# Attention outputs turned by DMA copies and normalised once an element, in place of transposes on TensorE; weights loaded after the first stacks

## The chip, the cores and the metric

The kernel runs on one core of one Trainium2 chip. The metric is the time of one execution on the device in microseconds (us). Beside it stand the times of several runs of the kernel before, and one execution that the hardware profiler recorded.

## What is computed

Eight elements (b) each go through a grouped-query cross attention and then through a recurrent block. Cut to what matters here:

```python
# attention: x (8,256,256), ctx (8,1601,256); 32 query heads, 8 key heads, 8 channels a head
q = (x @ Wq + bq).reshape(b, l, 8, 4, 8).transpose(0, 2, 3, 1, 4)
k = (ctx @ Wk + bk).reshape(b, s, 8, 8).transpose(0, 2, 1, 3)      # v in the same way
scores = einsum('bkgld,bksd->bkgls', q, k) / sqrt(8) + mask
attn = softmax(scores, axis=-1)
out = einsum('bkgls,bksd->bkgld', attn, v).transpose(0, 3, 1, 2, 4).reshape(b, l, 256)
x = layernorm(out @ Wo + bo + x) * gamma + beta
# block: layer norm, token shift, five mixes, r k v w g, a scan over 256 tokens
#   s = k v^T + w s   (32 heads of 8x8),  o = r (u k v^T + s),
# group norm, gate, Wo, layer norm, and a gated square-relu feed-forward
```

## The kernel before, in words

**Stages.** Elements are pipelined. `elements(it, lo)` gives for each turn `it` of the outer loop the elements f = it+2 (its context and queries are projected), a = it+1 (its values are turned, its keys and queries are stored to DRAM and loaded back as stacks), b = it (its scores, exponentials and weighings), c = it-1 (output projection and the first part of the recurrent block) and d = it-2 (feed-forward). There are ten turns; the first has no c, in the last two no b. On each engine the order of the work in a turn is written out by hand; a turn has STEPS = 52 steps.

**Scores.** A step is one chunk of 128 keys (13 chunks) of one of four groups of eight heads. Per step TensorE makes two tiles of scores (`score_tile`), ScalarE takes their exponentials (`exp_tile`, 128x1024) and TensorE weighs them (`weigh`) into the one accumulator bank `po`: four products with `v_aug`, which has the 8 value channels and a column of ones for each of four key heads, so that rows 32j to 32j+7 of `po` are the weighed values of head j and row 32j+8 is the sum of the exponentials. In light steps (LIGHT, and all but two where there is no c) a weighing stands between two score tiles; in the others both weighings of the pair of steps stand together. Side work of the other elements is put behind each even step (`side`, `score_rows`).

**The output of a group.** At the end of each group (steps 13, 26, 39 and, for the last, step 0 of the next turn) VectorE copies `po` to `o_raw` (`keep_output`); the first weighing of the next group waits for it (`o_kept`). TensorE turns `o_raw` to rows of tokens with four transposes (`turn_output`, at steps 22, 28 and 42, and at step 0 of the next turn), and VectorE takes the reciprocals of the 16 sums and multiplies (`norm_output`: one reciprocal and four products) into `attn`. At step 2 of the next turn `attn` is turned back to channels by four transposes (`turn_rows`), VectorE copies it to `attn_t`, and at step 4 `product_rows(attn_t, w_o, ...)` is the output projection.

**VectorE's order around step 26.** State passes 0 to 3 of the recurrence (`state_pass`, a product and a scan each), the copy of r, `keep_output(b, 1)`, `rk`, state pass 4, `norm_output(b, 1)`, g, passes 5 and 6, `bias_kv(f, 0)`, pass 7. The key projections of element f are at steps 30, 32, 40 and 40 (`project_kv`); the second waits for `bias_kv(f, 0)`, since both use one bank.

**The SP queue.** SP issues nearly all DMAs, in this order in a turn: step 0 second half of the stacks of b and x_rows of c; step 4 the stores of the queries (12) and keys (6) of a; 12 the output; 14 the shift of b to DRAM and back; 18 `spread_v(c)`, eight transfers of 257 KB that repeat each value channel over a head; 20 `load_ctx(f)` (four) and `load_x_t(f)`; 26 the first stacks of a; 38 the shift of a; 44 the mask of f. Each of these waits for what it needs, and what stands behind it waits too.

**The start.** `project` on ScalarE, with VectorE, splits keys and queries of element 0 in three bf16 parts; SP stores the keys and one half of the queries, ACT's queue the other half (`store_queries`), and both load half of the first stack. Then come a short scoring round, the shift to DRAM and back, and the first scores. SP loads the context and x of element 1 as soon as those of element 0 are projected. GpSimd issues 46 loads of weights (`late`) once the first context has landed; they are first needed in the second turn.

## Time and profile before

| | |
|---|---|
| median of 3 runs | 1179.3 us (1173.62 to 1179.63) |
| profiled execution | 1178.83 us |
| its span, first to last instruction | 1176.9 us |
| TensorE (PE) busy | 1054.9 us, 90% |
| ScalarE (ACT) busy | 860.3 us, 73% |
| VectorE (DVE) busy | 574.8 us, 49% |
| GpSimd (POOL) busy | 309.0 us, 26% |
| mean granted TensorE clock | 0.952 |

The shares are averages over a start of some 56 us without scores, eight turns with scores, and a tail in which the last element goes on alone. An engine's busy time counts compute instructions only. The chain that ended last lies on TensorE for 62% of the span, on ScalarE for 23%, on VectorE for 5% and on DMAs for 3%.

### The profile page before, as it was taken

The numbers are of one execution on the slowest core, as the hardware profiler recorded it, in microseconds if no ns is written. First come the engines' busy times: TensorE is split into PE (matmuls) and PEld (weight loads), VectorE is DVE, ScalarE is ACT, GpSimd is POOL, SyncE is SP. The second block draws the span as 40 slices with busy tenths as digits, with TensorE's granted clock in tenths as the row PEclk, the third lists the DMA queues.
The fourth block names the chain that finished last, engine by engine and source line by source line (L and its number), as shares of the span: only waits on it lengthen the run. The fifth ranks groups of instructions, "written<-read, shape, count | busy, mean of one in ns | idle before, by whom it ended". The sixth has DMA issues, their size and how long they took to land.

```text
span 1176.9 us, 18264 instructions
## 1 busy us (share of the span) xinstructions
PE 1054.9 (90%) x7181; PEld 376.0 (32%) x7181; DVE 574.8 (49%) x1095; ACT 860.3 (73%) x940; POOL 309.0 (26%) x356
## 2 busy tenths in 40 slices
PE   3198999999999999999999999999997999888777
PEld 2031223333333233323333333323331333224413
DVE  5031215464448445555547453844555364635562
ACT  2078988889878887888788988887788888881110
POOL 9221051232314041314123231314132012300330
PEclk8599999999999999999999999999999999998766
DMA  8534133631536140904253143614070225000400
GB/s 258 128 82 134 25 83 86 93 83 57 116 44 136 59 95 30 170 6 94 83 87 88 58 113 44 139 59 93 31 107 3 34 75 82 3 1 9 72 0 13
DMA packets 65374, 87.48 MB, mean 74 GB/s; under 512 B 8208, under 2 KB 48192, under 8 KB 65280
## 3 DMA queue, kind: packets, MB, share of 16 engines
q1 hardware_dynamic: 61728, 81.22, 31.6%
q0 software_dynamic: 2176, 4.11, 1.5%
q8 instruction: 59, 0.97, 0.3%
q10 hardware_dynamic: 1376, 0.90, 0.3%
q14 instruction: 35, 0.29, 0.1%
HBM read 50.74 MB, written 18.62 MB: 59 GB/s over the span
## 4 chain that ended last, share of the span: by engine, by line
PE 62%; ACT 23%; issue 6%; DVE 5%; DMA 3%; SPq 1%; POOL 0%; ACTq 0%; DVEq 0%; POOLq 0%
PE psum L795 61%; ACT probs L738 19%; DMA vs<-v_c 1%; DMA q_stacked<-q_parts 1%; ACT L738 1%; ACT L770 1%; PE psum L885 1%; SPq L291 1%; DVE xa L1336 1%; DMA q_stack<-q_stacked 1%; DVE row_max L1248 1%; DVE sx L1341 0%; ACT xm L767 0%; ACT xm L770 0%; SPq L367 0%
## 5 line engine op out<-in xcount | busy, mean ns | idle before, releaser
L738 ACT ACTIVATE probs<-psum 128x1024 f32<-128x1024 f32 (+1 forms) x832 | 798.9, 1022 | 199.8 <-PE psum L795 197.5
L795 PE MATMUL psum<-probs,v_aug 128*9 128x512 f32 (+1 forms) x3328 | 416.7, 599 | 1.3 <-DVE o_raw L1296 1.2
L795 PE MATMUL psum<-q_stack,k_stack 64*128 64x512 bf16 (+1 forms) x1745 | 320.5, 395 | 50.2 <-ACT probs L738 37.9
L795 PEld LDWEIGHTS psum<-q_stack,k_stack 64*128 64x128 bf16 (+1 forms) x1745 | 81.9, 96 | 440.5 <-ACT probs L738 359.5
L795 PEld LDWEIGHTS psum<-probs,v_aug 128*9 128x9 f32 (+1 forms) x3328 | 61.6, 89 | 161.2 <-issue 151.3
L599 POOL TENSOR_TENSOR vs<-r_c,vs 128x512 f32<-128x512 f32 x64 | 86.5, 1361 | 96.4 <-DVE tmp L1523 53.9
L576 POOL TENSOR_TENSOR xm<-tmp,xa 128x512 f32<-128x512 f32 x40 | 43.5, 1104 | 233.2 <-DVE tmp L1356 233.2
L1369 DVE TENSOR_TENSOR_SCAN vs<-w_c,vs 128x514 f32<-128x514 f32 x64 | 90.1, 1408 | 21.8 <-POOL vs L590 19.9
L563 POOL TENSOR_TENSOR rstd<-moments,eps 128x2 f32<-128x2 f32 x24 | 4.7, 195 | 255.8 <-DVE moments L1322 255.8
L1296 DVE COPY o_raw<-psum 128x512 f32<-128x512 f32 x32 | 21.9, 684 | 89.7 <-PE psum L795 89.7
L1362 DVE TENSOR_TENSOR vs<-k_c,vs 128x512 f32<-128x512 f32 x64 | 61.9, 967 | 0.3
L1356 DVE SCALAR_TENSOR_TENSOR tmp<-psum,chan,sx 128x256 f32<-128x256 f32 x80 | 33.5, 478 | 53.3 <-PE psum L795 53.3
L795 PE MATMUL psum<-ctx_t,w_kv 128*128 128x400 f32 (+1 forms) x128 | 50.1, 529 | 5.4 <-DMA ctx_t<-in_ctx_t 5.4
L535 POOL CAST k_parts<-kv 64x1601 bf16<-64x1601 f32 x7 | 10.6, 1519 | 121.0 <-DVE kv L1225 121.0
L1248 DVE TENSOR_REDUCE row_max<-psum 128x16 f32<-128x512 f32 x32 | 20.6, 684 | 41.8 <-PE psum L795 41.8
L1225 DVE TENSOR_SCALAR kv<-psum,b_kv 128x400 f32<-128x400 f32 (+1 forms) x28 | 17.6, 627 | 42.5 <-PE psum L795 42.5
L795 PE MATMUL psum<-k_stack,q_stack 48*128 48x32 bf16 x512 | 9.0, 174 | 30.9 <-DMA q_stack<-q_stacked 30.9
L795 PEld LDWEIGHTS psum<-ctx_t,w_kv 128*128 128x128 f32 x128 | 23.3, 195 | 25.2 <-issue 11.1
L1566 DVE RECIPROCAL xm<-xm 128x512 f32<-128x512 f32 x8 | 26.8, 3348 | 7.1 <-ACT xm L770 7.1
L1242 DVE TENSOR_REDUCE mask_max<-ctx_t 128x1 f32<-128x1601 f32 x16 | 28.7, 1806 | 0.0
L795 PE MATMUL psum<-mix,w 128*128 128x256 f32 (+1 forms) x64 | 18.0, 415 | 6.2 <-DVE mix L1345 6.2
L1285 DVE CAST shift_parts<-psum 32x128 bf16<-32x128 f32 x16 | 4.5, 279 | 38.8 <-PE psum L795 38.8
(181 smaller groups left out, 1061.8 us busy)
## 6 DMA issues: line engine op xcount, KB each, us to landing
vs<-v_c SPq DMA_DIRECT2D x61, 257.0 KB, 7.6
ctx_t<-in_mask SPq DMA_DIRECT2D x8, 1601.0 KB, 6.7
k_stacked<-k_parts SPq DMA_DIRECT2D x48, 200.1 KB
ctx_t<-in_ctx_t SPq DMA_DIRECT2D x24, 400.0 KB, 6.1
k_stack<-k_stacked SPq DMA_DIRECT2D x31, 300.2 KB, 6.6
q_stack<-q_stacked SPq DMA_DIRECT2D x31, 192.0 KB, 7.1
q_stacked<-q_parts SPq DMA_DIRECT2D x90, 64.0 KB, 3.1
ctx_t<-in_ctx_t SPq DMA_DIRECT2D x8, 401.0 KB, 6.4
```

Of the source, the lines that this page charges most:

```text
L576: nc.gpsimd.tensor_tensor(xm[MIX_ORDER[n]][:, :, :], tmp[n % 2][:, :, :], xa[:, :, 1:L + 1], ALU.add)\
L599: nc.gpsimd.tensor_tensor(vs[:, j, :, 0:L], r_c[:, :, :], vs[:, j, :, 0:L], ALU.mult)\
L738: nc.scalar.activation(probs[turn_step % NP][t][0:w, :, :], ps[t][0:w, :, :], ACT.Exp).then_inc(exped.sem, 1)
L795: return nc.tensor.matmul(dst, lhsT, rhs, start=start, stop=stop)
L1225: nc.vector.tensor_scalar(kv32[:, at:at + w], bank(at_bank)[:, 0:w], b_kv[:, 0:1], None, ALU.add)\
L1242: nc.vector.tensor_reduce(mask_max[:, a, lc:lc + 1], ctx_t[:, lc, :], AX.X, ALU.max, apply_absolute_value=True).then_inc(mask_seen.sem, 1)
L1248: last = nc.vector.tensor_reduce(row_max[:, :].rearrange("p (r a u) -> p r a u", a=2, u=4)[:, :, half, :], bank(6 + half).rearrange("p (r ...
L1296: nc.vector.tensor_copy(o_raw[:, :], po).then_inc(o_kept.sem, 1)
L1356: last = nc.vector.scalar_tensor_tensor(tmp[n % 2][:, e, :], halves(at)[:, e, :], vec(f"s{f}", e), sx[:, e, :], ALU.add, ALU.mult)
L1362: nc.vector.tensor_tensor(vs[:, j, :, 1:L + 1], k_c[:, :, :], vs[:, j, :, 1:L + 1], ALU.mult)\
L1369: nc.vector.tensor_tensor_scan(flat, w_c[:, :, :].rearrange("p e l -> p (e l)"), flat, 0.0, ALU.mult, ALU.add)\
L1566: link(nc.vector.reciprocal(std_o[:, :, :], std_o[:, :, :]))
```

## The change

1. `turn_output`, `norm_output`, the turning of `attn` and the copy to `attn_t` go. After each `keep_output`, SP copies each head's eight rows of `o_raw` to `attn_t`, laid by channels, and its row of sums, repeated eight times, to `den_t` (`turn_attn`: eight DMAs a group, at steps 22, 30 and 42, and the last at step 0 of the next turn, ahead of the stacks).
2. VectorE normalises once an element, at the head of the turn (`norm_attn`: a reciprocal, a minimum for the check of small sums, and a product, all 128x512), and the output projection at step 4 waits for it.
3. `keep_output` of a group waits for the copies of the group before it out of `o_raw`.
4. Waits on TensorE that stood for the removed work are put on what is next in those banks. LIGHT gets steps 22 and 28.
5. x_rows is loaded at step 46 of the turn before. `w_o` is loaded in eight pieces in the new order of channels.
6. At the start, the 53 loads of weights are issued after the first stack has landed, and the context and x of element 1 after SP's half of the first stack. Of the second half of the queries, two of six stores go to ACT's queue.

```diff
-LIGHT = (2, 8, 10, 18, 38, 42, 48)
+LIGHT = (2, 8, 10, 18, 22, 28, 38, 42, 48)
+ATTN_STEP = (22, 30, 42)
+FIRST_STORES = 2
...
+            wo_attn = c["L0_xattn_Wo"].rearrange("(g j u h d) n -> g u h j d n", g=GQ, j=4, u=2, h=GQ)
+            for group in range(GROUPS):
+                for h in range(GQ):
+                    yield w_o[32 * group:32 * group + 32, h, :], wo_attn[group // 2, group % 2, h]
...
+            def turn_attn(b, group):
+
+                if group == 0 and b > 0:
+                    sp.wait_ge(wo_done.sem, wo_done.at(b - 1))
+                sp.wait_ge(o_kept.sem, o_kept.at(b, group + 1))
+                for j in range(4):
+                    p0 = 32 * group + HD * j
+                    for dst, src in ((den_t, o_raw[32 * j + HD:32 * j + HD + 1, :].rearrange("p (a n) -> p a n", a=1)
+                                      .broadcast_to([1, HD, 512])),
+                                     (attn_t, o_raw[32 * j:32 * j + HD, :])):
+                        sp.dma_start(dst[p0:p0 + HD, :, :].rearrange("p h l -> p (h l)"), src).then_inc(attn_in.sem, 16)
...
-                sp.wait_ge(kv_proj.sem, kv_proj.at(lo))
-                load_ctx(lo + 1)
-                sp.wait_ge(q_proj.sem, q_proj.at(lo))
-                load_x_t(lo + 1)
...
                 store_k_parts(lo)
-                store_q_parts(lo, (1,))
+                sp.wait_ge(q_low.sem, q_low.at(lo))
+                store_queries(sp, lo, 1, range(FIRST_STORES, NR))
                 load_stacks(lo, 0, (0,))
+                sp.wait_ge(kv_proj.sem, kv_proj.at(lo))
+                sp.wait_ge(q_proj.sem, q_proj.at(lo))
+                load_ctx(lo + 1)
+                load_x_t(lo + 1)
...
                         if step == 0:
+                            if c is not None:
+                                turn_attn(c, 3)
                             if b is not None:
                                 load_stacks(b, 1)
-                            if c is not None:
-                                load_x_rows(c)
+                        if step in ATTN_STEP and b is not None:
+                            turn_attn(b, ATTN_STEP.index(step))
+                        if step == 46 and b is not None:
+                            load_x_rows(b)
...
+                if lo == 0:
+                    pool.wait_ge(stack_in[0].sem, stack_in[0].at(0))
+                    for dst, src in late:
+                        pool.dma_start(dst, src).then_inc(late_in.sem, 16)
...
-            pool.wait_ge(ctx_in[NK - 1].sem, ctx_in[NK - 1].at(0))
-            for dst, src in late:
-                pool.dma_start(dst, src).then_inc(late_in.sem, 16)
...
                 store_queries(act, a, 0)
+                store_queries(act, a, 1, range(FIRST_STORES))
...
             def keep_output(b, group):
                 dve.wait_ge(weighed.sem, weighed.at(b, NC * (group + 1)))
-                dve.wait_ge(o_turned.sem, o_turned.at(b, group))
+                if group > 0:
+                    dve.wait_ge(attn_in.sem, attn_in.at(b, 16 * HD * group))
+                elif b > 0:
+                    dve.wait_ge(attn_in.sem, attn_in.at(b - 1))
                 nc.vector.tensor_copy(o_raw[:, :], po).then_inc(o_kept.sem, 1)
...
+            def norm_attn(b):
+
+                dve.wait_ge(attn_in.sem, attn_in.at(b))
+                nc.vector.reciprocal(den_t[:, :, :], den_t[:, :, :]).then_inc(den_turned.sem, 1)
+                dve.wait_ge(den_turned.sem, den_turned.at(b))
+                nc.vector.tensor_reduce(den_low[:, b % B:b % B + 1], den_t[:, :, :], AX.XY, ALU.min)
+                nc.vector.tensor_tensor(attn_t[:, :, :], attn_t[:, :, :], den_t[:, :, :], ALU.mult)\
+                  .then_inc(attn_normed.sem, 1)
```

## Rows read from the trace of the kernel before

**Rows 1.** Windows, one element: us, busy (instructions) of each engine, clock, DMA share, GB/s

```profile
371.96:499.62 127.66, 123.59 (x888) 44.77 (x889) 69.94 (x137) 106.64 (x117) 34.85 (x37) 1.00 0.38 83
```

**Rows 2.** Groups of instructions by shape, whole span: busy us, mean ns, idle before

```profile
L885 PE MATMUL psum<-ident,o_raw 128*128 128x128 f32 x128 | 20.6, 283 | 0.4 <-DVE o_raw L1296 0.4
...
L1310 DVE TENSOR_TENSOR attn<-psum,r_den 128x32 f32<-128x32 f32 x128 | 15.5, 184 | 1.1
...
L1303 DVE RECIPROCAL r_den<-psum 128x16 f32<-128x16 f32 x32 | 7.8, 245 | 31.0 <-PE psum L885 31.0
...
L891 PE MATMUL psum<-ident,attn 128*128 128x128 f32 x32 | 5.2, 286 | 1.8 <-DVE attn L1310 1.8
```

**Rows 3.** Timeline of TensorE in one element: start us, us, what

```profile
379.30 1.61 PE L795 MATMUL psum<-ctx_t,w_kv 128*128 128x400 f32 x4
...
406.46 0.39 PE L795 MATMUL psum<-q_stack,k_stack 64*128 64x512 bf16 x2 [0.22 <-ACT probs L738]
...
438.29 1.99 PE L795 MATMUL psum<-w_o,attn_t 128*128 128x256 f32 x8
...
484.40 0.66 PE L885 MATMUL psum<-ident,o_raw 128*128 128x128 f32 x4
484.99 0.70 PE L795 MATMUL psum<-q_stack,k_stack 64*128 64x512 bf16 x4
...
495.30 1.91 PE L795 MATMUL psum<-probs,v_aug 128*9 128x512 f32 x16
```

**Rows 4.** Timeline of VectorE in the same element

```profile
378.57 0.61 DVE L1225 TENSOR_SCALAR kv<-psum,b_kv 128x401 f32<-128x401 f32 x1
...
401.34 3.34 DVE L1566 RECIPROCAL xm<-xm 128x512 f32<-128x512 f32 x1
...
427.70 0.69 DVE L1296 COPY o_raw<-psum 128x512 f32<-128x512 f32 x1 [4.39 <-PE psum L795]
...
440.75 0.69 DVE L1460 TENSOR_TENSOR x<-psum,x_rows 128x512 f32<-128x512 f32 x1 [2.30 <-PE psum L795]
...
492.56 0.68 DVE L1296 COPY o_raw<-psum 128x512 f32<-128x512 f32 x1
```

**Rows 5.** Timeline of the SP queue in the same element

```profile
469.88 14.85 SPq L304 DMA_DIRECT2D vs<-v_c  x8
484.85 4.73 SPq L351 DMA_DIRECT2D ctx_t<-in_ctx_t  x4
489.62 0.58 SPq L354 DMA_DIRECT2D x_t<-in_x_t  x1
```

**Rows 6.** DMA issues from 470 to 498 us: KB each, us to landing

```profile
x_t<-in_x_t SPq DMA_DIRECT2D x1, 256.0 KB, 7.6
```

**Rows 7.** DMA issues of the whole span: count, KB each, median us to landing

```profile
q_stacked<-q_parts SPq DMA_DIRECT2D x90, 64.0 KB, 3.1
...
shift_stacked<-shift_parts SPq DMA_DIRECT2D x16, 24.0 KB, 1.4
```

**Rows 8.** Timeline of all engines at the start, 0 to 62 us

```profile
10.85 0.93 POOL L681 DMA_DIRECT2D w_o<-in_L_xattn_Wo  x1 [0.32 <-POOL q_stack L677]
...
19.76 4.10 ACTq L291 DMA_DIRECT2D q_stacked<-q_parts  x6
...
22.89 8.75 SPq L291 DMA_DIRECT2D q_stacked<-q_parts  x6
...
35.86 0.54 POOL L681 DMA_DIRECT2D s_init<-in_s_init  x1
...
39.85 0.35 SPq L284 DMA_DIRECT2D k_stack<-k_stacked  x1
...
47.02 0.61 PE L795 MATMUL psum<-k_stack,q_stack 48*128 48x32 bf16 x32 [30.92 <-DMA q_stack<-q_stacked]
...
51.28 0.30 SPq L385 DMA_DIRECT2D shift_stacked<-shift_parts  x1
...
56.12 1.04 PE L795 MATMUL psum<-q_stack,k_stack 64*128 64x512 bf16 x4 [6.25 <-issue]
```

**Rows 9.** Timeline of all engines where the last element's scores end

```profile
1065.17 0.69 DVE L1296 COPY o_raw<-psum 128x512 f32<-128x512 f32 x1 [3.60 <-PE psum L795]
...
1070.66 3.78 PE L795 MATMUL psum<-w_o,attn_t 128*128 128x256 f32 x8 [0.78 <-DVE attn_t L1452]
```

More of the change, by code:

```diff
@@ L880, in weigh @@
                 last.then_inc(weighed.sem, 1)
-            def turn_output(b, group, to):
-                pe.wait_ge(o_kept.sem, o_kept.at(b, group + 1))
-                for u in range(4):
-                    last = nc.tensor.transpose(bank(to)[:, P * u:P * u + P], o_raw[:, P * u:P * u + P], ident[:, :])
-                last.then_inc(o_turned.sem, 1)
             def turn_rows(x, to, done):
@@ L1124, in side @@
                         if n == 0:
-                            pe.wait_ge(o_normed.sem, o_normed.at(b, 2))
+                            if c is not None:
+                                pe.wait_ge(k_ready.sem, k_ready.at(c))
+                            else:
+                                pe.wait_ge(v_kept.sem, v_kept.at(a))
                         elif n == 1:
@@ L1508, in all_turns @@
                         mix_of(c, 4)
-                    if b is not None:
-                        norm_output(b, 0, 6)
                     if c is not None:
@@ L1526, in all_turns @@
                         state_pass(c, 4)
-                    if b is not None:
-                        norm_output(b, 1, 5)
                     if c is not None:
@@ L1573, in all_turns @@
                           .then_inc(og_ready.sem, 1)
-                    if b is not None:
-                        norm_output(b, 2, 5)
                     if c is not None:
```

83 lines of the change are left out of this document (17 added, 66 removed).

## Prediction

> **What bounds the kernel now.** I read the busy time by stretch first, one stretch per element, then the waits inside one, then the timelines of TensorE, VectorE, the SP queue, and last the start and the end. One element takes 127.66 us, in which TensorE is busy 123.59 and ScalarE 106.64, at a granted clock of 1.00 [rows 1]. So TensorE sets the pace, with short stretches in which it waits for an exponential instead, as in [rows 3] before 406.46. The reader is to see two kinds of time there: a TensorE instruction taken out of the first kind is worth its length, one out of the second is worth nothing. The program's own time for the profiled execution is 1178.83 us, the span 1176.9; the sum below is made against 1178.83, which lies 0.5 under the median of the runs, 1179.3.
>
> Names: "round 1 to 5" are the turns of the outer loop in which an element's scores, the tail of the one before and the projection of the one two ahead all run; rounds 6 and 7 lack the projection; the first turn is round 0; the tail follows round 7. Steps of one round lie as in [rows 3]: step 0 near 425, step 28 near 495, steps 30 and 32 near 375 and 379 (add 127.66 to set them behind step 28).
>
> **Turning removed from TensorE.** Four blocks of four transposes of o_raw and one block of attn an element: 128 cost 20.6 us and 32 cost 5.2 [rows 2], 0.64 us a block, and the timeline advances by about 0.53 where a block goes. The blocks at steps 0, 22 and 28 stand where TensorE is never idle (the one at 484.40 is followed at once by scores, [rows 3]): 3 x 0.53 = 1.6 us an element. The blocks at steps 2 and 42 are followed by a wait for ScalarE (the one before 406.46), so they give nothing. In round 0, with light steps only, I take nothing. Steps 22 and 28 become light; their side work falls to about 1.1 us, and the finer order only makes sure that the 0.53 is reaped. Bound: 0 to 0.3 more a step. Without any new wait this is 1.6 in each of seven rounds.
>
> **Normalising on VectorE.** Removed: 4 x (0.245 + 4 x 0.121) [rows 2] and one copy of 0.69, together 3.6 us an element. Added, all at once at the head of a round: a reciprocal of 128x512, 3.34 us by the one at 401.34, a minimum and a product of that width, 0.69 each by the 440.75 one [rows 4]: 4.7 us. VectorE has room for it (busy 69.94 of 127.66, [rows 1]); what matters is who waits.
>
> **The head of a round (steps 0 to 4).** o_raw is copied at 427.70 to 428.39 [rows 4]. SP must then issue eight DMAs of 16 KB (8 partitions of 512 f32). No such copy is in the trace; the nearest issue rows are 0.30 us (51.28) and 0.35 us (39.85) and, for sixteen-partition ones, 0.68 (six in 4.10) [rows 8]; I take 0.4, which gives 431.7. Landing: 1.4 us by the shift rows, 3.1 by the query stores [rows 7]; with the queue else empty I take 2 from the start of the last issue, 433.3. Then 4.7 on VectorE: 438.1. TensorE wants attn_t at 438.29 - 0.53 = 437.8 [rows 3], so it waits 0.4 and the step-0 gain shrinks to 0.1. Bounds: issue 0.3 and landing 1.4 leave no wait; 0.68 and 3.1 give 3.7 us of wait each round. Behind the waiting product stands all of TensorE's queue. x0's addition (440.75) and what follows it keep their time, since SP's later items, the loads of the second stacks and eighteen stores, move by some 8 us where they have 10 or more to spare.
>
> **The copies at step 22: the heart of the forecast.** The first group's o_raw is ready early in the round, but SP runs in order, and its copies stand behind the eight spread transfers (469.88, 14.85 us of issuing) and the loads of the next context and x (484.85 and 489.62) [rows 5]. So the first of the eight is issued at 490.2, the last near 493.6. The second group's keep_output is now made to wait for them, and before it ran at 492.56 [rows 4]. The load of x issued at 489.62 took 7.6 us to land, at 497.2 [rows 6]. If the small copies queue behind it they land near 497.6: VectorE is late by 5.0 us. Behind keep_output there stand rk, state passes 4 to 7 and the bias of the next keys; behind rk, GpSimd's products. TensorE wants the freed accumulator for the weighing at 495.30 [rows 3], minus 0.5 to 0.8 by the gains and the lighter step; it stops until 498.3, 3.5 us. The second half of VectorE's lateness shows at step 32: the key projection at 379.30 [rows 3] waits for the bias that ends at 378.57 + 0.61 = 379.18 [rows 4], 0.12 us before it. VectorE has lost 5.0 and saved one norm_output since (0.7), so that bias comes 4.4 later, and TensorE, its gains at 22 and 28 swallowed, is 4.3 later than before. Lower bound: copies that land 2 us after the last issue, 495.5, make VectorE late by 2.9 and the round 2.1 longer. Upper: landing at 499.5 gives 6.2. I take 4.3, as the nearest row is a transfer on the same queue issued 0.6 us earlier. In rounds 6 and 7 no context is loaded: copies are issued from 484.85 and, 7.6 behind the last spread issue near 482.9, land near 490.5, in time, and steps 22 and 28 gain 0.5 each. In round 0 nothing is spread and there is no wait.
>
> By the page "DMA: Bandwidth & Descriptors" of the Trainium skill, section "Queues, rings and completion order", each engine takes the descriptors of a ring in order, yet "completion is not FIFO per issuing engine", and a DMA uses at most sixteen rings. The trace has landings in order of issue, but no copy of eight partitions. Were these small copies to overtake, the rounds would cost the 2.1 of the lower bound and the sum would be that of rival B.
>
> **The other copies.** Groups 1 and 2 are asked for half a round after they are issued, and x_rows moves to step 46, all with over 10 us to spare: nothing.
>
> **The start.** The first scores come at 56.12 [rows 8]. Before that the query stores on SP take 8.75 us for six, where ACT's six took 4.10 (0.68 each), while GpSimd's loads run until 35.86 + 0.54; the stack loads go out at 39.85 and are used at 47.02. After: SP has four stores and ACT eight, so both are issued by 22.9 + 2.7 = 25.6; landing 3.1 [rows 7] gives 28.7, 11.1 us sooner. The stacks then share the engines with the next context, behind SP's half: 1 us lost. The round trip of the shift (51.28 to 56.12, 4.8 us) now meets that context and the late weights: 0.6 us lost. Gain 9.5; bounds 4 and 12. GpSimd's 53 loads (0.55 each, as 46 ran from 10.85 to 36.4 [rows 8]) start near 36.5 and end near 66, before q_scaled lets it go on near 69: hidden; without that cover they cost nothing until the stores of step 8 are late by over 5 us.
>
> **The tail.** No score work covers the last element. o_raw is copied by 1065.86, the product ran at 1070.66 [rows 9]. After: 8 x 0.4 + 1.6 + 4.7 + 0.1 = 9.6 (terms as at the head of a round), so 1075.5: 4.8 lost, bounds 3.5 and 8. The flag check loses two 512-wide instructions, hidden behind the spread.
>
> **Sum.** Start -9.5; round 0, 0; rounds 1 to 5, 5 x (4.3 - 0.1) = +21; rounds 6 and 7, 2 x (-1.0 - 0.1) = -2.2; tail +4.8. Together +14.1: 1178.8 + 14.1 = 1193.
>
> **Rivals.**
> A, faster: no wait at step 22, because the DMAs land before 492.6. It is decided at that point: with SP issuing from 490.2 it needs the spread or the context to be issued 3 us faster than in [rows 5]. -9.5 - 7 x 1.1 + 4.8 = -12.4: 1166.
> B, a short wait: the copies land 2 us after their issue, despite the context. -9.5 + 5 x (2.1 - 0.1) - 2.2 + 4.8 = +3.1: 1182.
> C, the start gives little: late weights delay the shift's two hops and the stacks, gain 4 rather than 9.5: 1198.
> D, the head of the round becomes a wait too: issue at 0.68 and landing 3.1 add 3.3 to each of seven rounds: 1216. The order of SP speaks against: nothing is queued ahead then.
>
> **Chances.** Forecast 0.46, A 0.18, B 0.19, C 0.10, D 0.07. Within 0.5% is about what a measurement of this kernel can tell from no change: 1173.4 to 1185.2. Faster is A with a little of B (0.20); same is most of B and the low edge of the forecast (0.20); slower 0.60. The range 1166 to 1203 takes in B, C, the upper stall of 6.2 (1203) and half of A; the forecast's own is 1185 to 1203.
>
> **What would show it.** o_raw's second copy in a round on VectorE should follow a DMA, 4 to 6 us of idle; TensorE idle before the first weighing of group 2, about 3.5 us, and at the key projection of step 32, under 1; five rounds near 131.9 us, then two near 126.5. The first scores should start near 46.5. The last attn_t product should come some 10 us after o_raw. If the rounds are 126.5 throughout, the queue argument is wrong; if the first scores come after 52, the start is.

## Result and the profile after

The changed kernel takes 1224.05 us (median, 1221.41 to 1225.63), the kernel before, run beside it, 1179.47. The ratio is 1.0383, interval 1.0351 to 1.0415: slower by 3.8%. Forecast was 1193.0 with a range to 1203: the sign was right, the size a third of what came (14.1 us for 42.3 between the two profiled executions, 44.6 between the medians). The profiled execution of after took 1221.41 us with a span of 1219.2, 42.3 more than the span before.

First the windows of one element (round 3), cut at VectorE's four copies into `o_raw`; columns as in [rows 1]:

```profile
440.84:477.04 36.20, 31.54 (x249) 11.93 (x249) 23.17 (x45) 27.93 (x32) 6.03 (x8) 1.00 0.43 96
477.04:512.95 35.91, 32.38 (x214) 12.88 (x214) 14.97 (x24) 27.43 (x31) 7.01 (x7) 0.99 0.64 120
512.95:545.54 32.59, 31.27 (x220) 7.76 (x220) 18.60 (x25) 24.82 (x27) 11.94 (x12) 0.90 0.22 34
545.54:576.15 30.61, 29.05 (x190) 10.18 (x190) 15.31 (x27) 26.56 (x29) 11.23 (x10) 1.00 0.21 67
```

The same four stretches of before, 427.70 to 555.36, are 34.60, 30.26, 32.19 and 30.61 us long. The element has grown from 127.66 to 135.31, and the growth sits in two stretches: the first one, where VectorE normalises, and above all the second, which ends when the second copy into `o_raw` can start.

That second stretch on the SP queue:

```profile
484.61 14.76 SPq L306 DMA_DIRECT2D vs<-v_c  x8
499.49 4.95 SPq L356 DMA_DIRECT2D ctx_t<-in_ctx_t  x4
504.48 0.55 SPq L359 DMA_DIRECT2D x_t<-in_x_t  x1
505.13 0.86 SPq L416 DMA_DIRECT2D den_t<-o_raw  x1
...
510.14 0.63 SPq L416 DMA_DIRECT2D attn_t<-o_raw  x1
```

and who waits for it, on VectorE and then on TensorE:

```profile
506.65 0.67 DVE L1498 COPY r_c<-psum 128x512 f32<-128x512 f32 x1
512.95 0.69 DVE L1291 COPY o_raw<-psum 128x512 f32<-128x512 f32 x1 [5.63 <-DMA attn_t<-o_raw]
```

```profile
509.28 0.39 PE L819 MATMUL psum<-q_stack,k_stack 64*128 64x512 bf16 x2
513.79 1.89 PE L819 MATMUL psum<-probs,v_aug 128*9 128x512 f32 x8 [4.11 <-DVE o_raw L1291]
```

The eight copies of the first group stand behind spread, context and x, as forecast from [rows 5]; each holds SP for 0.63 us and they start 0.67 apart. The x just ahead of them was issued at 504.48 and took 7.6 us to land, so it landed at 512.1 (DMA issues, 495 to 520: KB each, us to landing):

```profile
x_t<-in_x_t SPq DMA_DIRECT2D x1, 256.0 KB, 7.6
```

The copies landed by 512.95, 2.8 us behind the start of the last issue. VectorE's wait is 5.40, 5.85, 5.63, 4.82 and 4.87 us in rounds 1 to 5 (forecast 5.0), and 1.35 and 1.30 in rounds 6 and 7 (forecast none). TensorE's stop is 3.88, 4.33, 4.11, 3.30 and 3.35 us in rounds 1 to 5 (forecast 3.5). In rounds 4 and 5 TensorE waits once more, for the bias of the keys at step 32, as the prediction had it (forecast under 1); here round 4:

```profile
661.52 1.61 PE L819 MATMUL psum<-ctx_t,w_kv 128*128 128x400 f32 x4 [0.22 <-DVE kv L1217]
```

The head of the round, on VectorE:

```profile
440.84 0.69 DVE L1291 COPY o_raw<-psum 128x512 f32<-128x512 f32 x1 [4.39 <-PE psum L819]
...
448.30 3.35 DVE L1296 RECIPROCAL den_t<-den_t 128x512 f32<-128x512 f32 x1 [3.61 <-DMA attn_t<-o_raw]
```

and on TensorE, behind the minimum and the product that follow it:

```profile
453.03 1.99 PE L819 MATMUL psum<-w_o,attn_t 128*128 128x256 f32 x8 [1.96 <-DVE attn_t L1299]
```

SP's issues run from 441.56 to 446.93 and the reciprocal starts at 448.30: 2.0 us behind the start of the last issue, as assumed, but eight issues took 5.4 us and not 3.2. So here too TensorE stops, 1.96 us a round where 0.4 was forecast; 3.02 in round 1 and 2.45 in round 7.

The clock of TensorE in the stop and behind it (windows; columns as in [rows 1]):

```profile
509.00:513.00 4.00, 0.67 (x4) 0.10 (x2) 0.05 (x1) 1.27 (x2) 0.00 (x0) 0.94 0.53 142
513.00:515.00 2.00, 1.21 (x8) 0.16 (x8) 2.00 (x4) 0.00 (x0) 0.49 (x1) 0.50 1.14 191
515.00:517.00 2.00, 2.00 (x12) 0.26 (x12) 0.03 (x1) 0.73 (x1) 2.00 (x2) 0.50 1.13 178
517.00:519.00 2.00, 2.00 (x11) 0.16 (x3) 1.56 (x1) 1.70 (x3) 2.00 (x4) 0.50 0.96 129
```

After the stop of round 3 the granted clock is 0.50 (1.2 of 2.4 GHz) for some seven microseconds, and a block of eight weighings takes 1.89 us instead of 1.05. Behind the stops of rounds 1, 2, 4 and 5 half clock lasts some three and a half microseconds, and so it does behind TensorE's wait at the head of rounds 1, 2 and 7, where it follows waits of 3.02, 1.96 and 2.45 us; behind the waits of 1.95 and 1.96 us at the head of rounds 3 to 6 there is none. Before has no such stretch in its rounds 1 to 5. It looks like a second bill for the same stop, and nothing in the prediction speaks of it. The third experiment is about it.

The start, on TensorE:

```profile
38.67 0.61 PE L819 MATMUL psum<-k_stack,q_stack 48*128 48x32 bf16 x32 [21.45 <-DMA q_stack<-q_stacked]
...
50.92 1.04 PE L819 MATMUL psum<-q_stack,k_stack 64*128 64x512 bf16 x4 [9.41 <-issue]
```

The first stack is used 8.35 us sooner than in [rows 8], but the first scores come only 5.2 us sooner: the round trip of the shift, 4.8 us in [rows 8], now takes 8.0. The tail ends as follows (TensorE, the last element; the answer to [rows 9]); the last copy into `o_raw` began at 1104.02:

```profile
1116.19 3.78 PE L819 MATMUL psum<-w_o,attn_t 128*128 128x256 f32 x8 [10.31 <-DVE attn_t L1299]
```

Where the 42.3 us are, read from the starts of the fourth copy into `o_raw` of each element in the two traces:

```
                                 before            after            change   forecast
start and round 0 (to its copy)  174.60            169.47            -5.1     -9.5
rounds 1 to 5                    810.84 - 174.60   843.37 - 169.47   +37.7    +21
rounds 6 and 7                   1065.17 - 810.84  1104.02 - 843.37   +6.3    -2.2
tail                             1176.9 - 1065.17  1219.2 - 1104.02   +3.5    +4.8
```

Every row but the last missed on the side that makes the time longer.

### The profile page after: what moved, and what is told of

The parts are those of the page before. It is cut to its first block, busy times and chain, and to the rows that moved or that the text cites. A ratio compares the mean times of both kernels' runs of the same rounds, so it can differ in the third digit from the quotient of the medians.

```text
span 1219.2 us, 18031 instructions
## 1 busy us (share of the span) xinstructions
PE 1049.5 (86%) x7021; PEld 358.4 (29%) x7021; DVE 589.9 (48%) x951; ACT 860.3 (71%) x940; POOL 322.2 (26%) x363
## 4 chain that ended last, share of the span: by engine, by line
PE 46%; ACT 18%; issue 11%; SPq 9%; DVE 9%; DMA 4%; POOL 1%; ACTq 1%; POOLq 0%; DVEq 0%
PE psum L819 46%; ACT probs L762 15%; SPq L416 4%; SPq L306 4%; DVE den_t L1296 2%; DMA attn_t<-o_raw 2%; SPq L356 1%; DMA vs<-v_c 1%; ACT L762 1%; ACT L794 1%; DVE o_raw L1291 1%; ACTq L293 1%; DVE xa L1322 1%; DVE vs L1348 1%; DMA q_stack<-q_stacked 1%
## 5 line engine op out<-in xcount | busy, mean ns | idle before, releaser
L819 PE MATMUL psum<-probs,v_aug 128*9 128x512 f32 (+1 forms) x3328 | 427.3, 609 | 20.3 <-DVE o_raw L1291 20.2
L1355 DVE TENSOR_TENSOR_SCAN vs<-w_c,vs 128x514 f32<-128x514 f32 x64 | 102.3, 1598 | 21.9 <-POOL vs L612 20.0
L598 POOL TENSOR_TENSOR xm<-tmp,xa 128x512 f32<-128x512 f32 x40 | 46.0, 1166 | 235.0 <-DVE tmp L1342 235.0
L1348 DVE TENSOR_TENSOR vs<-k_c,vs 128x512 f32<-128x512 f32 x64 | 54.6, 853 | 0.3
L819 PE MATMUL psum<-w_o,attn_t 128*128 128x256 f32 x64 | 20.9, 481 | 25.6 <-DVE attn_t L1299 25.6
L1296 DVE RECIPROCAL den_t<-den_t 128x512 f32<-128x512 f32 x8 | 26.8, 3353 | 32.6 <-DMA attn_t<-o_raw 32.6
L1217 DVE TENSOR_SCALAR kv<-psum,b_kv 128x400 f32<-128x400 f32 (+1 forms) x28 | 17.6, 627 | 50.7 <-PE psum L819 50.7
L1546 DVE RECIPROCAL xm<-xm 128x512 f32<-128x512 f32 x8 | 26.8, 3347 | 7.1 <-ACT xm L794 7.1
L819 PE MATMUL psum<-k_stack,q_stack 48*128 48x32 bf16 x512 | 9.0, 174 | 21.5 <-DMA q_stack<-q_stacked 21.5
```

The source lines that it names most:

```text
L598: nc.gpsimd.tensor_tensor(xm[MIX_ORDER[n]][:, :, :], tmp[n % 2][:, :, :], xa[:, :, 1:L + 1], ALU.add)\
L819: return nc.tensor.matmul(dst, lhsT, rhs, start=start, stop=stop)
L1296: nc.vector.reciprocal(den_t[:, :, :], den_t[:, :, :]).then_inc(den_turned.sem, 1)
L1348: nc.vector.tensor_tensor(vs[:, j, :, 1:L + 1], k_c[:, :, :], vs[:, j, :, 1:L + 1], ALU.mult)\
L1355: nc.vector.tensor_tensor_scan(flat, w_c[:, :, :].rearrange("p e l -> p (e l)"), flat, 0.0, ALU.mult, ALU.add)\
```

## The experiments

The theory after this reading: the order of the SP queue makes the wait behind step 22; copies at 0.63 us each to issue make the wait at the head; the half clock behind the stop costs another 2 us a round; the shift's round trip at the start is slow by what is loaded beside it. Times are medians beside the kernel before on the same chip, whose median in the four series was 1177.97, 1178.45, 1178.93 and 1178.47 us. "First stretch" to "fourth stretch" of a round are those of the windows above. In rounds 1 to 5 of after they last 36.2 us (36.93 in round 1, 37.78 in round 2), 35.1 to 36.1, 31.7 to 31.9 (32.59 in round 3) and 30.60.

**1. The copies of the first group ahead of the spread.**

```
-ATTN_STEP = (22, 30, 42)
+ATTN_STEP = (16, 30, 42)
```

> The changed kernel with the copies of the first group issued at step 16 of the SP queue instead of step 22, so ahead of the spread transfers and the loads of the next context and x. Theory (the order of the SP queue makes the wait, and the stop of 4.1 us sends TensorE to half clock behind it): VectorE's second o_raw copy no longer waits for a DMA, TensorE's wait before the first weighing of group 2 and the half-clock stretch behind it both go, and rounds 1 to 5 become 6 to 7 us shorter, rounds 6 and 7 under 1: about 1190 us. Rival 1 (the wait costs only its own 4 us less the gains at steps 22 and 28; the clock has another cause): 5 x 3.5 less, about 1206. Rival 2 (the eight copies cost by their transfers and the extra VectorE work, wherever they stand): 1218 to 1224.

Measured: 1197.27 us, ratio 1.0167 (1.0122 to 1.0212), 26.8 less than after. SP now issues the eight copies from 466.15 on, before the spread, and VectorE's second copy has no wait:

```profile
494.88 0.68 DVE L1291 COPY o_raw<-psum 128x512 f32<-128x512 f32 x1
```

The second stretch is 30.20 us in rounds 1 to 6, the third 32.32, and the rounds are 129.3 to 130.0 us (one of them 131.0, with half clock in its head). Against the 133.6 of rounds 4 and 5 of after the step 22 term is 4.3 us, the number that the prediction gave it; by the second and third stretches of all of rounds 1 to 5 it is 5.0 on average. The time lies between the theory's 1190, which asked for 6 to 7 us a round, and rival 1's 1206, which asked for 3.5. Rival 2, that the copies cost by their transfers and by VectorE's work wherever they stand, is out. The third stretch is 0.6 longer than in rounds 4 and 5 of after, while the second lost 4.9 to 5.9: part of a stop is given back by the stretch behind it.

**2. Denominators first.**

```
-                for j in range(4):
-                    ...den_t copy j, attn_t copy j, both on attn_in
+                for j in range(4):  den_t copy j   .then_inc(den_in.sem, 16)
+                for j in range(4):  attn_t copy j  .then_inc(attn_in.sem, 16)
...
-                dve.wait_ge(attn_in.sem, attn_in.at(b))
+                dve.wait_ge(den_in.sem, den_in.at(b))
                 nc.vector.reciprocal(...)
                 ...
+                dve.wait_ge(attn_in.sem, attn_in.at(b))
                 nc.vector.tensor_tensor(attn_t ...)
```

> The changed kernel with the four denominator copies of a group ahead of the four value copies, on a signal of their own, so that the reciprocal (3.35 us) runs while the value copies are issued and land. Theory (attn_t is late by VectorE's 4.7 us behind eight slow issues): the product of attn_t finds its operand ready or waits under 0.5 us instead of 1.96 in the seven rounds, and the last one comes 3 us sooner in the tail: 7 x 1.5 + 3 = 13 less, about 1211. Rival (TensorE's wait at step 4 is given back later in the round by a wait for ScalarE or for the step 22 copies): only the tail's 3 us, about 1221.

Measured: 1202.05 us, ratio 1.0194 (1.0147 to 1.0242): 22 less than after, more than the 13 expected. On VectorE at the head of round 3:

```profile
437.90 3.35 DVE L1300 RECIPROCAL den_t<-den_t 128x512 f32<-128x512 f32 x1 [1.13 <-DMA den_t<-o_raw]
```

and on TensorE, with no wait:

```profile
443.09 1.99 PE L821 MATMUL psum<-w_o,attn_t 128*128 128x256 f32 x8
```

The first stretch falls from 36.18 to 34.17, 2.0 us, so the whole wait at the head went into the round and nothing gave it back; in rounds 1, 2 and 7 it falls by 4.1, 3.6 and 3.4, since the wait is 3.02 in the first and 2.45 in the last and half clock stood behind the wait in all three. The waits behind step 22 are as before the edit (4.75 to 5.64). The heads together are 19.2 us shorter, against the 10.5 that I had put on them: I had counted part of a wait that was wholly on the path.

**3. The stop filled with work.** Sixteen matmuls, whose result is not used, ahead of the weighing that waits.

```
+                            if step == 28 and c is not None and f is not None:
+                                pe.wait_ge(k_ready.sem, k_ready.at(c))
+                                for _ in range(16):
+                                    mm(bank(5), k_stack[1][0:HALF, 0, 0:P], q_stack[1][0:HALF, 0, 0:2, :])
```

> The changed kernel with sixteen matmuls of 64x512 whose result is never used, added on TensorE at step 28 of rounds 1 to 5, just ahead of the weighing that waits 4.1 us; they only fill the wait. Theory (the half clock behind the stop is the stop's own consequence, and costs 2 to 2.5 us a round): granted clock 0.9 or more in the six us behind the wait, x8 weighing back near 1.05 us, the wait itself ended at the same time by the same o_raw copy: 10 to 12 less, about 1213. Rival 1 (the clock falls for the work of the round as a whole): the clock stays at 0.5 there and the time is within 2 us of 1224. Rival 2 (fillers last longer than the wait): slower, up to 1230.

Measured: 1225.81 us, ratio 1.0417 (1.0362 to 1.0471): no gain. The fillers did what they were to do. TensorE in round 3, and two windows behind the wait:

```profile
506.43 3.84 PE L819 MATMUL psum<-q_stack,k_stack 64*128 64x512 bf16 x18
510.65 1.05 PE L819 MATMUL psum<-probs,v_aug 128*9 128x512 f32 x8 [0.38 <-DVE o_raw L1295]
...
515.46 0.39 PE L819 MATMUL psum<-q_stack,k_stack 64*128 64x512 bf16 x2 [0.53 <-ACT probs L762]
...
523.89 1.61 PE L819 MATMUL psum<-ctx_t,w_kv 128*128 128x400 f32 x4 [1.02 <-DVE kv L1221]
```

```profile
511.00:513.00 2.00, 2.00 (x20) 0.23 (x12) 0.89 (x2) 0.94 (x2) 1.62 (x2) 1.00 1.19 145
513.00:515.00 2.00, 1.94 (x10) 0.49 (x6) 0.70 (x1) 2.00 (x4) 2.00 (x3) 1.00 1.10 147
```

The clock is 1.00, the weighing is back at 1.05, and yet the third stretch is 31.69 us, as in rounds 4 and 5 of after (31.70, 31.69). TensorE, faster there, waits 0.53 us for an exponential and then 1.02 us for the bias of the keys at step 32 (0.73 in round 1, 1.02 to 1.04 in the others). That is the second half of VectorE's lateness: the projection starts 14.08 us behind the start of VectorE's second copy, and it does so in rounds 4 and 5 of after too (647.43 to 661.52), where the clock was at 0.50 on the way. So my theory of a second bill has fallen: the half clock is the stop's consequence, as the fillers show, but VectorE's chain from that copy to the bias sets the pace there. Some three and a half microseconds of half clock cost 0 to 0.2 us of the third stretch; the seven of round 3 cost 0.9 (32.59), as in rounds 3 to 5 of experiment 2 (32.54 to 32.74). Half clock did cost up to 1.6 us where it lay in a first stretch: 37.78 instead of 36.18 in round 2 of after, and three heads of 37.77 to 37.83 in this run, which took back what the third stretches gained.

**4. What a copy costs to issue.** Fourteen DMAs added behind everything else, each issued when the one before has landed; forms in the order 8 rows, one row onto 8, 16, 32, 64, 128 rows, 8 rows of 64 elements.

> The changed kernel with fourteen single DMAs added on SP behind everything else, two of each form, each landed before the next: o_raw's 8 rows of 512 f32 into attn_t, one row broadcast to 8, then 16, 32, 64 and 128 rows, and 8 rows of 64. Theory (issuing costs by the number of rows, so of descriptors, with a base): 8 rows 0.63 us as in the rounds, 128 rows well over 1. Rival (issuing costs by the DMA alone for copies between two tiles on chip, whatever their rows): 0.6 to 0.65 for every form, in which case one copy of 32 or 128 rows would do for a quarter of the price. Landing near 2 us for all up to 16 rows by either.

Measured: 1248.72 us in one run, longer by the added DMAs. Rows of their line on the SP queue, duration in ns and start (the second of 8 rows, of 16 rows, of 128 rows, and of 8 rows of 64):

```profile
L542 SPq DMA_DIRECT2D attn_t<-o_raw x1: 670/670/670, 1219.4 to 1219.4; - x1
...
L542 SPq DMA_DIRECT2D attn_t<-o_raw x1: 540/540/540, 1227.8 to 1227.8; - x1
...
L542 SPq DMA_DIRECT2D attn_t<-o_raw x1: 465/465/465, 1240.4 to 1240.4; - x1
...
L542 SPq DMA_DIRECT2D attn_t<-o_raw x1: 679/679/679, 1244.4 to 1244.4; - x1
```

My theory of a price by rows fell: 256 KB in 128 rows hold SP for 0.47 us, 2 KB in 8 rows for 0.68. The price is one for each DMA, and among these forms it is the higher the fewer the partitions (one row onto eight 0.63, 32 rows 0.51). From the issue of the second copy of its form to the next issue, with the landing between, pass 2.1 us for 8 rows and 2.3 for 128.

**5. Fewer issues: one copy for a group's four denominators.**

```
+                dens = o_raw[HD:P:32, :].rearrange("p (a n) -> p a n", a=1).broadcast_to([4, HD, 512])
+                sp.dma_start(den_t[32 * group:32 * group + 32, :, :]..., dens).then_inc(attn_in.sem, 16)
                 for j in range(4):  attn_t copy j
```

> The changed kernel with one DMA for the four denominators of a group (rows 8, 40, 72 and 104 of o_raw, each spread over eight) instead of four, so five copies a group instead of eight, nothing else. The probe found that issuing such a copy costs 0.47 to 0.80 us whatever its rows, the smallest the most. Theory (it is the number of issues that counts): three issues fewer are 2.0 us; TensorE's wait for attn_t goes (1.96), the one behind step 22 falls by 2 (4.1 to about 2), the tail by 2: 5 x 4 + 2 x 3.3 + 2 = 28 less, about 1196. Rival (the transfers, not the issues, make the time from o_raw to attn_t): within 3 of 1224.

Measured: 1219.19 us, ratio 1.0333 (1.0302 to 1.0363). Half of the theory held: the first stretch is 34.16, the wait at the head gone, and rounds 6 and 7 have no wait behind step 22. The other half failed, on VectorE in round 3:

```profile
513.10 0.69 DVE L1291 COPY o_raw<-psum 128x512 f32<-128x512 f32 x1 [8.46 <-DMA attn_t<-o_raw]
```

SP issued these five copies from 502.44 to 506.09, behind the x at 501.68, which took 9.5 us and so landed at 511.2. They landed only at 513.1: seven microseconds behind the end of their last issue, against two behind its start at the head. With the context and x in flight it isn't the issues that set the landing. That the wait even grew (8.5 for 5.4) may come from the stacks, 984 KB in four loads, which are now issued at 506.25 and share the engines with x and copies; this is argued, no run isolates it.

**6. One store and two loads through DRAM.**

```
-                for j in range(4): ...eight copies
+                sp.dma_start(o_st_d[group], o_raw[:, :]).then_inc(attn_out.sem, 16)
+                sp.wait_ge(attn_out.sem, attn_out.at(b, 16 * (group + 1)))
+                heads = o_st_d[group].rearrange("(j q) n -> j q n", q=32)
+                ...den_t from heads[:, HD:HD + 1, :] eightfold, attn_t from heads[:, 0:HD, :]
-                    dve.wait_ge(attn_in.sem, attn_in.at(b, 16 * HD * group))
+                    dve.wait_ge(attn_out.sem, attn_out.at(b, 16 * group))
```

> The changed kernel with each group's o_raw stored whole to DRAM in one DMA and brought back by two (the four denominators, each spread over eight partitions, and the 32 rows of values), all on SP at the same steps; VectorE's next copy waits for the store alone. Theory (issues and what stands ahead of them set the wait, not the bytes): VectorE's wait behind step 22 is under 1.5 us instead of 5.3 and TensorE's at attn_t under 0.5 instead of 1.96: about 40 less, 1184. Rival (the 256 KB store is served after the context and x loaded ahead of it on the same queue and lands 5 us or more after its issue): the wait behind step 22 stays at 3 or more, 1200 or above.

Measured: 1223.82 us, ratio 1.0367 (1.0323 to 1.0411). The rival. SP and VectorE in round 3:

```profile
505.11 0.49 SPq L360 DMA_DIRECT2D x_t<-in_x_t  x1
505.70 0.96 SPq L412 DMA_DIRECT2D o_stacked<-o_raw  x1
513.93 0.72 SPq L416 DMA_DIRECT2D den_t<-o_stacked  x1
```

```profile
514.00 0.69 DVE L1292 COPY o_raw<-psum 128x512 f32<-128x512 f32 x1 [6.09 <-DMA o_stacked<-o_raw]
```

One issue instead of eight, over by 506.7, and VectorE goes on 8.3 us behind its start, where the median landing of all such stores is 3.6. In the other rounds VectorE waits 4.3 to 4.7. At the head the two hops cost no less than the eight issues did (waits of 1.5 to 3.1 us at `attn_t`, 4.1 in round 1).

**7. Behind the spread, ahead of the context.**

```
-ATTN_STEP = (22, 30, 42)
+ATTN_STEP = (19, 30, 42)
```

> The changed kernel with the first group's copies at step 19 of the SP queue: behind the eight spread transfers as before, but ahead of the loads of the next context and x. Five copies instead of eight did not shorten VectorE's wait behind step 22 (8.5 us), nor did one store of the whole tile (4.6), so the theory is now: these copies land when the context and x that were issued ahead of them have landed, whenever their own issue ends. Theory: issued from 499.5, eight in 5.4 us, landed 2 later, at 507: as wanted at 507.3, so the wait is under 0.5 and the time that of the step 16 kernel, 1197. Rival (what is ahead on the queue at all, the spread too, holds them): wait 2 or more, 1205 to 1215.

Measured: 1200.95 us, ratio 1.0214 (1.0178 to 1.025): by the theory, with a rest for the rival. The SP queue and VectorE in round 3:

```profile
487.64 1.93 SPq L416 DMA_DIRECT2D den_t<-o_raw  x1
489.61 1.90 SPq L416 DMA_DIRECT2D attn_t<-o_raw  x1
491.55 0.63 SPq L416 DMA_DIRECT2D den_t<-o_raw  x1
...
495.65 1.93 SPq L356 DMA_DIRECT2D ctx_t<-in_ctx_t  x4
```

```profile
496.96 0.69 DVE L1291 COPY o_raw<-psum 128x512 f32<-128x512 f32 x1 [1.58 <-DMA attn_t<-o_raw]
```

The last of the eight is issued at 494.91, so the landing is back at 2 us behind it, and the wait at 1.1 to 1.6 us for 4.8 to 5.9. So some three quarters of the wait came of standing behind the context and x, and a quarter of the place behind the spread: the first two copies hold SP for 1.9 us each, and the four context loads, 4.95 us behind the spread in after, are now issued in 1.93. This run doesn't part two things that the context and x do to the copies. Issuing the loads ahead holds SP for 5.5 us in after, and their transfers delay the landing; by experiments 5 and 6 earlier issue without the second is not enough.

**8. The start alone, on the kernel before.** The late weights behind the first stack, four query stores on SP and eight on ACT, context and x behind the stack; nothing of the attention part.

> The kernel before with only the changes of the start: the late weights behind the first stacks on the GpSimd queue (in one piece for Wo, as before), four query stores on SP and eight on ScalarE, the next context and x loaded behind the stacks. Theory (the start is worth 5.2 us, of the 9.5 forecast, because the shift's round trip takes 8.0 instead of 4.8): first scores near 51, 1174 us. Rival (the start alone is worth nearly the 9.5; what ate it are the thirty-two small Wo loads of the change): first scores near 47.5, 1170.

Measured: 1174.53 us, ratio 0.9971 (0.9956 to 0.9985); first scores at 51.27, the fourth copy into `o_raw` at 170.44 for 174.60. The rival is out: the small pieces of `w_o` don't matter, and the start is worth 4 to 5 us in either kernel.

**9. What delays the shift.** The late weights wait for the shift instead of the stack:

```
-                    pool.wait_ge(stack_in[0].sem, stack_in[0].at(0))
+                    pool.wait_ge(shift_in[0].sem, shift_in[0].at(0))
```

> The changed kernel with the late weights waiting for the shift of the first stack to have come in, not for the stack. Theory (the round trip of the shift, 42.93 to 50.92, is slow because the late weights go out at 38.84 ahead of it): round trip back near 5 us, first scores near 48, 3 less: 1221. Rival (it is the context and x of the next element, on the same SP queue just ahead of the shift): unchanged, 1224.

and, beside that, context and x moved on SP from behind the stack to behind `shift_to_stack`:

> As the one with the late weights behind the shift, and the next context and x loaded behind the shift as well. By either theory of the start the round trip is now alone: 4.8 us or less, first scores near 47.5, about 1220. Beside the other it tells the share of the context. If the first scores stay at 51, neither is the cause.

Measured: 1225.64 us (1.0427, 1.0399 to 1.0456) and 1228.36 (1.0436, 1.0415 to 1.0457). First scores at 47.36 and 47.14, so 3.6 us sooner than in after and another 0.2. The round trip of the shift is 4.74 and 4.68 us, for 7.99 in after: the late weights are 3.3 us of it, the context 0.1 at most, and the rest is a first stack that came 0.3 sooner. But neither kernel is faster. By the fourth copy into `o_raw` they stand at 172.59 and 172.11, where after is at 169.47: all and more is given back within round 0. The second of them on GpSimd, VectorE and TensorE:

```profile
76.68 0.52 POOL L546 COPY v_aug<-v_st 128x384 f32<-128x384 f32 x1
```

```profile
77.44 0.69 DVE L1226 COPY v_st<-psum 128x512 f32<-128x512 f32 x1 [6.75 <-POOL v_aug L550]
```

```profile
78.65 0.56 PE L819 MATMUL psum<-k_stack,q_stack 48*128 48x32 bf16 x32 [1.51 <-DVE v_st L1230]
85.88 0.63 PE L819 MATMUL psum<-ident,neg_shift 128*32 128x128 f32 x2 [3.56 <-DVE neg_shift L1267]
```

GpSimd issues the 53 loads in one piece, some 29.3 us, and its first copy of the values of element 1, at 68.17 in after, stands behind them. VectorE waits for that copy, and TensorE for VectorE. The prediction had priced this cover: nothing until the loads are late by over 5 us. Here the copy behind them is 8.5 later, and what stops TensorE is that copy and not the stores.

**10. The late loads in GpSimd's idle time.** On the kernel before, with the start of 8, context and x behind the shift, and the late loads issued behind the second copy of V in the first turn (46 of them, since this kernel loads `w_o` in one piece):

```
                         copy_v(a, 0)
+                    if it == 0:
+                        for dst, src in late:
+                            pool.dma_start(dst, src).then_inc(late_in.sem, 16)
```

> The kernel before with the start of the change made better: query stores split over SP and ScalarE, the next context and x behind the shift, and the fifty-three late loads put into GpSimd's idle time behind the second copy of V in the first turn (its rows before show it idle from 119.5 to 150.9) rather than ahead of the first one. With the loads merely behind the shift, GpSimd's first copy of V came 8.5 us later (76.68) and TensorE stopped for it, which took back 6.4 of the 9. Theory: first scores at 47.2 and round 0 as long as before, 118.5, so 8.9 less: 1170. Rival (the time returns at another place of the first turn, for the late weights' preparation): o_raw's fourth copy at 170 or later, 1174.5 as with the start alone.

Measured: 1168.70 us, ratio 0.993 (0.9905 to 0.9954): faster than both kernels, by 0.7% against before. First scores at 46.73, the fourth copy into `o_raw` at 165.47, 9.1 sooner than before; GpSimd issues from 110.29 to 135.9 and has 5.87 us left before its next work. The forecast's 9.5 for the start was there to be had, in another place of the queue.

**11. All in one.** Step 16, denominators first, and the start of 9 with both edits:

> Step 16 for the first group's copies, denominators first, and the late weights, context and x behind the shift, all in one. Theory: the gains add, 33 + 13 + 4: about 1174, at or a little under the kernel before (1179), since each round is then 1 us shorter than before by the removed transposes. Rival (the wait moves on to the copies of group 1 or 3, or the gains at the steps are not real): 1183 or more.

Measured: 1179.63 us, ratio 1.0018 (1.0000 to 1.0035), the time of before. That is neither the theory's 1174 nor the rival's 1183. Rounds 2 to 5 are 127.28 us against 127.66, so there the removed transposes are worth 0.38 us a round, not 1.6; rounds 1 and 7 are 0.6 and 0.7 longer than before.

**12. Was it the finer order?** On the kernel of 11:

```
-LIGHT = (2, 8, 10, 18, 22, 28, 38, 42, 48)
+LIGHT = (2, 8, 10, 18, 38, 42, 48)
```

> The kernel that has all four edits (step 16, denominators first, late weights and context behind the shift), with steps 22 and 28 taken out of LIGHT again, as before. Its rounds are 127.28 us, where the removed transposes (three blocks of 0.53 that TensorE had no idle time beside) should have left 126.1. Theory (the finer order at steps 22 and 28 costs TensorE what the transposes gave, about 0.4 a step): rounds near 126.4, 7 x 0.8 less: 1174. Rival (ScalarE's exponentials set the pace as soon as the transposes go): rounds still 127.3, 1179.6.

Measured: 1180.59 us, ratio 1.0034 (1.0015 to 1.0053), rounds of 127.22 us. The rival. TensorE at step 28, before and then here:

```profile
497.67 0.65 PE L885 MATMUL psum<-ident,o_raw 128*128 128x128 f32 x4
498.16 1.02 PE L795 MATMUL psum<-tmp,same 128*128 128x512 f32 x2
499.12 0.89 PE L795 MATMUL psum<-q_stack,k_stack 64*128 64x512 bf16 x4
```

```profile
494.97 1.13 PE L821 MATMUL psum<-tmp,same 128*128 128x512 f32 x2
496.03 0.39 PE L821 MATMUL psum<-q_stack,k_stack 64*128 64x512 bf16 x2
496.92 0.39 PE L821 MATMUL psum<-q_stack,k_stack 64*128 64x512 bf16 x2 [0.50 <-ACT probs L764]
```

The four transposes (0.53 of advance) are gone and TensorE waits 0.50 us for an exponential in their place; at step 22 of this run there is a new wait of 0.50 too. Over round 3 of the kernel of 11 TensorE is busy 121.79 us of 127.28, before 123.59 of 127.66 [rows 1]: of 1.80 us of work taken away, 1.42 came back as idle time. ScalarE was right behind it.

**13. The change with everything mended.** As 11, with the late loads placed as in 10:

> The kernel that has all four edits, with the late loads in GpSimd's idle time of the first turn instead of behind the shift. Theory: o_raw's fourth copy at 166 instead of 172.05, everything behind it unchanged: 6 less, 1173.5. Rival: unchanged, 1179.6.

Measured: 1173.12 us, ratio 0.9959 (0.9938 to 0.998), 0.4% faster than before and 0.4% slower than the kernel of experiment 10, which leaves the attention part alone. Rounds are 127.28; what the attention part still costs is in the main the tail, in which TensorE waits 7.84 us for `attn_t` where before it waited 0.78 [rows 9] and the product starts 9.7 us behind the start of the copy instead of 5.5.

## Why the prediction was right in sign and wrong in size

The miss is 42.3 - 14.1 = 28.2 us. Cut by the stretches of the two traces it is: the heads of seven rounds 18.3 (first stretches +17.6 for -0.7), step 22 in rounds 1 to 5 3.8 (second and third stretches +25.3 for +21.5), the rest of rounds 6 and 7 3.1, the start 4.4, the tail -1.3.

**Step 22, +4.3 a round: right in mechanism and nearly in size.** The wait of VectorE was 5.3 on average for 5.0, TensorE's stop 3.8 for 3.5, the term 4.3 and 4.4 in rounds 4 and 5, and 5.1 to 6.1 in the first three. The second half of the lateness, a wait for the bias at step 32, came too: 0.22 and 0.16 us in rounds 4 and 5, none in rounds 1 to 3, where half clock had made TensorE late itself, and 0.7 to 1.0 with the clock kept up (experiment 3). That the number fits so well is in part luck: with the last copy issued at 510.14, two microseconds of landing alone would have given 512.1, the very time at which the x landed, so after itself can't tell the queue from the slow issue. The copies did queue behind the load of x, and rival B, the short wait, would have needed them to land without regard to it: experiments 5 and 6 issued them earlier or as one, and they still landed 7 to 8 us behind their issue; 7 put them ahead of the context and they landed in 2. The "DMA: Bandwidth & Descriptors" page of the Trainium skill, section "Queues, rings and completion order", allows a later DMA to complete first; no run here showed these copies overtaking the x. Rounds 6 and 7 wait too, 1.3 us, since with 0.67 an issue instead of 0.4 the last of eight is issued 2 us later than assumed; the third stretch gives that back.

**Head of the round, -0.1: the step that failed most, really +1.4 to +1.6 in rounds 3 to 6, and +4.6, +3.2 and +3.7 in rounds 1, 2 and 7.** The landing of 2 us was right, and so was the gain at step 0 (0.44 for 0.53, by the first stretches of 34.16 and 34.60 in experiment 11 and before). The issue was 0.67 from one copy to the next and not 0.4, so that eight took 5.4 us and not 3.2, and TensorE waits 2.0 where 0.4 was put. The rows had both prices: 0.30 and 0.35 from the shift and the stack, 0.68 from the query stores. The value between leaned to the wrong row, and rival D, which had the 0.68, asked for a slow landing too and was put at 0.07, since nothing is queued ahead then. One half of the rival was enough.

**Transposes at steps 22 and 28, -0.5 each: they gave nothing.** "The blocks at steps 0, 22 and 28 stand where TensorE is never idle", so their 0.53 was taken whole. A stretch without idle time shows which engine is the bound now, not by how much: ScalarE's exponentials were 0.5 us behind, and that is what TensorE waits for in their place (experiments 11 and 12). In rounds 1 to 5 the stop swallowed the gain in the sum anyway, so this is only 2 us of the miss, in rounds 6 and 7; but it is why the mended change hardly gains.

**Start, -9.5: really -5.1.** The query stores were issued by 30.0 and not 25.6: the six key stores ahead of SP's share took 6.3 us, until 25.3, and ACT's eight took 9.1. The late weights put 3.3 us on the shift's round trip where 0.6 was allowed for them and the context (experiment 9). This was rival C. 4.4 of the miss.

**Tail, +4.8: really +3.5**, although the product came later than forecast, 12.2 us behind the start of the copy (forecast 10.3, before 5.5). The 1.9 more is the issue price again. From the product to the end after has 103.0 us and before 106.2, but the runs of experiments 8 and 10, whose tail is the code of before, have 103.2 and 103.1 there: the 3.2 that came back is a difference between executions and no effect of the change. That the tail came in under its forecast is luck.

**Half clock: put at nothing, really some 5 of the 28.2.** The prediction says nothing of TensorE's clock behind a wait. Half clock lies in the heads of rounds 1, 2 and 7 and costs some 4 us there by the first stretches of experiment 2, and about 1.2 us behind the five stops, 0.9 of it in round 3 (experiment 3). These microseconds are part of the terms above and not a further one. Not every such stretch hangs on a stop of this change: the kernel of experiment 8 has one in its round 6, where the third stretch is 33.85 us for 32.20. Chances: "slower" had 0.6 and came; the range's upper end of 1203 took the cases one by one, while here D's half, C and the overrated gain came together.

## What to carry to other kernels

Work taken from the busiest engine is worth its length only down to the next engine's pace; read how idle that one is in the same stretch before counting it. A small transfer with a consumer belongs ahead of bulk loads in its queue, and its place counted for more here than its number of pieces; with an empty queue it is the other way round, and each piece costs its issue. Before loads are moved on an engine that also computes, look up its next instruction, who waits for it, and where the engine is idle anyway.

## What the runs showed of the hardware

Issuing a small copy between two tiles on chip holds SP for 0.63 to 0.68 us, and a copy of 128 rows for 0.47 (experiment 4). Here eight took 5.4 us to issue and the last landed 2 us after its start. The "DMA: Bandwidth & Descriptors" page of the Trainium skill, section "Issuing engines are not separate DMA queues", says that the time to initiate a DMA is usually small relative to the DMA itself; for pieces of 16 KB these rows have 0.67 of some 2.1 us, about a third, and with eight in a row the issuing is the larger part.

The first two issues directly behind the spread transfers last 1.9 us each for copies that else take 0.63 (experiment 7). Four context loads took 4.95 us to issue at that place in after, and 1.93 away from it.

A small VectorE instruction was held up by a long one of GpSimd. In the kernel of experiment 9 with both edits, VectorE and GpSimd:

```profile
87.54 2.99 DVE L1281 CAST shift_parts<-shift_rest 32x128 bf16<-32x128 f32 x1
```

```profile
87.44 3.01 POOL L567 TENSOR_TENSOR k_parts<-k_rest,k_parts 64x1601 bf16<-64x1601 f32 x1
```

The same cast took 0.21 us in after, at 87.97, when GpSimd's instruction had ended. It ends here 0.08 us behind GpSimd's, which had started 0.10 us before it. The page "SBUF — State Buffer" of the Trainium skill, section "SBUF: two separate sides", tells of a port pair that the two engines hold as an exclusive lock for a whole instruction; by that rule, these rows agree.
